# Attention on 32-row float32r slices instead of 128-row bfloat16 pieces, in a transformer block on one core

## The chip, the cores and the metric

The kernel runs on one core of one Trainium2 chip. The metric is the device time in microseconds of one execution; three runs of the kernel before gave 805.25 (median), 802.18 and 806.52.

## What is computed

One block with adaptive layer normalisation, on an input of 2 sequences x 1024 tokens x 128 features, all in float32. Cut to what matters here:

```
h = layernorm(x) * (1 + ca) + sa
q = h @ wq;  lat = h @ w_down;  k = lat @ wk_up;  v = lat @ wv_up      # 16 heads of 8
q, k = rope(q), rope(k)
scores = q . k / sqrt(8)
allowed = page(key) <= page(query)                                     # pages of 32 tokens
attn = softmax(where(allowed, scores, min))
x = x + ga * ((attn @ v) @ wo)
h = layernorm(x) * (1 + cb) + sb
x = x + gb * more_ffn(h)     # 4 rounds of top-2 routing over 4 experts, 128 -> 512 -> 128, gelu
```

The result must be close to float32, so products that the kernel runs at a lower precision are put together from pieces: a number is split into a rounded part and what is left over, and the products of the pieces are added up.

## The kernel before, in words

The kernel has four blocks, one behind the other, with all engines meeting in between: `prep` (line 171), `attention` (421), `project` (753), `ffn` (869). Each engine runs its own written-out order and waits on semaphores.

**prep** goes over four chunks of 512 tokens. TensorE makes q and k (and each with its feature pairs swapped, for the rotation), VectorE rotates them (355 to 362), and ScalarE and GpSimd split each into three bfloat16 pieces: first piece by ScalarE (258), rest by GpSimd (294), second piece by ScalarE (262), third by GpSimd (300). The SP queue stores the three pieces of each side and chunk in DRAM (227), and after the second chunk loads the first two head groups back (`load_group`, 161) in the layout that attention wants, six transfers a group. The block ends when all stores have landed (234).

**attention** works on 8 groups: 2 sequences x 4 groups of 4 heads (`HG`). For each head the 128 rows of the tiles `qs` and `ks` hold six pairs of pieces (`Q_PIECE`, `K_PIECE`; 48 rows), zero rows, 32 rows that mask pages, and 3 rows for the maximum, so one matmul over 128 rows gives masked scores less the row's maximum. Three streams run side by side:

- *Maxima.* For each head, 10 "bins" of up to 512 keys (`BINS`, 61) are filled by TensorE (`fill_bin`, 704: queries on partitions) into one of three banks `mx`, and VectorE reads each with one reduction (588). When a group's 40 bins are read, VectorE merges and splits the maxima in six small steps (602 to 612), TensorE turns them (713), VectorE copies them out (621), and one DMA (498) puts them into the maxima rows of `qs`.
- *Scores and exponentials.* 9 units a group (`UNITS`, 44), each 512 queries wide against one or two key blocks. TensorE makes the scores of each head with keys on partitions (660) into a ring of three banks `st`; ScalarE takes the exponential (562) into `probs`.
- *Values.* TensorE multiplies `probs` with `vs` (681), four heads in four column groups of 32, in float32, in two halves of 256 columns for each unit, into two output banks `ov`; ScalarE copies a finished bank out (568). `vs` has a column of ones, so the sum of the exponentials comes with it.

The order on TensorE is in `body` (724): for each half unit, the scores of two heads of the next unit, a quarter of a part of the bins, the values of half the present unit, the next quarter. The bins run 13 units ahead of the scores (a whole group and `LEAD` = 4), so 57 bins come before the first score. The loop over groups is a hardware loop of two rounds of three groups, with the last two groups written out. SP waits for the first maxima row, issues it, then the feed-forward weights and small tables, then the loads of the third group; later, in each group, a group's loads and a maxima row (500). GpSimd splits the feed-forward weights (539 to 543) and stages `vs`.

Of the kernel before, what the change touches and what calls it, by code (L numbers as in the profile page):

```python
# [32 lines left out]
Q_PIECE = [0, 0, 0, 1, 1, 2]  # L33
K_PIECE = [0, 1, 2, 0, 1, 0]
TERMS = len(Q_PIECE)
ROW_ZERO = TERMS * D
ROW_PAGE = 64
ROW_MAX = P - 3
NPAGE = T // PAGE
MASKED = -3.0e38  # L40
# [4 lines left out]
    [(0, 0, 0, 0, 512)],  # L45
    [(1, 0, 0, 0, 512)],
    [(0, 2, 0, 256, 256), (1, 6, 256, 256, 256)],
    [(0, 1, 0, 128, 384), (0, 3, 384, 384, 128)],
    [(1, 1, 0, 0, 512)],
    [(1, 2, 0, 0, 512)],  # L50
    [(1, 3, 0, 0, 512)],
    [(1, 4, 0, 0, 512)],
    [(1, 5, 0, 128, 384), (1, 7, 384, 384, 128)],
]
NU = len(UNITS)
FIRST_UNIT = [0, 1]
LAST_UNIT = [3, NU - 1]
# [15 lines left out]
GROUP_BINS = [(h, n) for h in range(HG) for n in range(len(BINS))]  # L73
NBINS = len(GROUP_BINS)
NB = NBINS + 1
LEAD = 4
CHAIN = 6
TURN_AFTER = 7
PARTS = [GROUP_BINS[u * NBINS // NU:(u + 1) * NBINS // NU] for u in range(NU)]
BEFORE = [u * NBINS // NU for u in range(NU)]  # L80

# [17 lines left out]
def adaln_block(nc, w, out):  # L99

    with ExitStack() as stack:
# [4 lines left out]
        m.qp = nc.dram_tensor("q_pieces", (3, GROUPS, HG * D, T), BF16).ap()  # L106
        m.kp = nc.dram_tensor("k_pieces", (3, GROUPS, HG * D, T), BF16).ap()
        m.x = m.sb("x_sb", [P, NT, E])
        m.ident = m.sb("ident", [P, P])
        m.identb = m.sb("identb", [P, P], BF16)  # L110
# [19 lines left out]
        with ExitStack() as upto_attention:  # L130
            ma = Mem(nc, upto_attention)
            m.v = ma.sb("v_all", [P, GROUPS, JB, HG * D])
            m.ks = [ma.sb(f"ks{s}", [P, HG, T], BF16) for s in range(SLOTS)]
            m.qs = [ma.sb(f"qs{s}", [P, HG, T], BF16) for s in range(SLOTS)]
# [23 lines left out]
LOADS = [(0, 3), (3, 2), (5, 1)]  # L158


def load_group(sp, m, g, s):

    for first, n in LOADS:
        rows = slice(first * D, (first + n) * D)
        sp.dma_start(m.ks[s][rows, :, :],
                     m.kp[0:n, g].rearrange("c (d h) t -> c d (h t)", d=D)).then_inc(m.qk_in[s], 16)
        one = m.qp[Q_PIECE[first]:Q_PIECE[first] + 1, g].rearrange("c (d h) t -> c d (h t)", d=D)
        sp.dma_start(m.qs[s][rows, :, :], one.broadcast_to([n, D, HG * T])).then_inc(m.qk_in[s], 16)


def prep(nc, m, l):
# [18 lines left out]
    rr = [l.sb(f"rr{s}", [P, CH]) for s in "qk"]  # L190
# [17 lines left out]
    with nc.Block() as block:  # L208

        @block.sync  # L210
        def _(sp):
# [8 lines left out]
            for c in range(NCH):  # L220
# [8 lines left out]
                if c == 1:  # L229
                    sp.wait_ge(pieces_out, 16 * 4)  # L230
                    load_group(sp, m, 0, 0)
                    load_group(sp, m, 1, 1)
# [971 lines left out]
```

## Time and profile before

| | before |
|---|---|
| runs: median (lowest to highest) | 805.25 us (802.18 to 806.52) |
| profiled execution: span from first to last instruction | 804.3 us |
| mean granted TensorE clock | 0.947 |
| TensorE busy | 720.4 us (90%) |
| VectorE busy | 595.7 us (74%) |
| ScalarE busy | 551.1 us (69%) |
| GpSimd busy | 190.9 us (24%) |
| moved by DMA | 20.06 MB |

The profile gives no time of the profiled execution but its span. The stages follow from the first and last instructions of each block: prep to 74 us, attention to 340, projection to some 360, feed-forward to the end. In the rows, PE is TensorE (PEld its weight loads, a line of their own because they overlap the matmuls), DVE VectorE, ACT ScalarE, POOL GpSimd, SPq the DMA-issuing queue of the sync engine. A float32 matmul stands as two records, and matmul ends are modelled, so the starts are what to read.

### The profile page before, as it was taken

How to read it: one execution, taken by the hardware profiler on the slowest of the kernel's cores; microseconds unless marked ns; L12 is line 12 of the kernel's file. 1: busy time of each engine (PE TensorE's matmuls, PEld its weight loads, DVE VectorE, ACT ScalarE, POOL GpSimd, SP SyncE). 2: the span in 40 equal slices, each digit the busy share in tenths (PEclk: the TensorE clock that was granted, in tenths of full speed). 3: DMA queues.
4: the chain of work that ended last, by engine and by line, in shares of the span. 5: the costliest groups of instructions: out<-in, count | busy, mean ns of one | idle time of the engine just before them, and what ended most of it. 6: DMA issues, size and time to landing. Idle time of an engine off the chain costs nothing.

```text
span 804.3 us, 14061 instructions
## 1 busy us (share of the span) xinstructions
PE 720.4 (90%) x4265; PEld 453.4 (56%) x4265; DVE 595.7 (74%) x1148; ACT 551.1 (69%) x958; POOL 190.9 (24%) x152
## 2 busy tenths in 40 slices
PE   4912897999899999977999999999999999999998
PEld 2400132333333333355777777877787777777786
DVE  5752986888688884095687788777887788777876
ACT  2520054766577768825888888888888888888884
POOL 0541033000000000002233333332333333332333
PEclk9965588999999999996999999999999999999999
DMA  9531040110110100000000000000000000000001
GB/s 239 158 119 50 0 131 22 40 38 12 37 30 15 40 4 2 2 1 0 1 2 1 0 1 0 0 0 0 0 0 0 0 0 0 0 0 0 0 0 52
DMA packets 14580, 20.06 MB, mean 25 GB/s; under 512 B 2794, under 2 KB 10474, under 8 KB 13766
## 3 DMA queue, kind: packets, MB, share of 16 engines
q1 hardware_dynamic: 13221, 17.74, 7.4%
q10 hardware_dynamic: 1312, 1.74, 0.8%
q8 instruction: 26, 0.43, 0.2%
q14 instruction: 21, 0.16, 0.1%
HBM read 15.08 MB, written 4.19 MB: 24 GB/s over the span
## 4 chain that ended last, share of the span: by engine, by line
PE 47%; issue 3%; DVE 2%; ACT 1%; POOL 0%; POOLq 0%; DVEq 0%
PE y L951 8%; PE y L953 7%; PE y L952 7%; PE hid L939 7%; PE hid L941 7%; PE hid L940 7%; PE pcw L969 4%; PE plog L959 2%; ACT gel_hi L1011 1%; DVE cw L1086 0%; DVE cw L1084 0%; DVE gel_lo L1042 0%; POOL cur L1135 0%; POOL cur_lo L1123 0%; DVE hdiff L1076 0%
## 5 line engine op out<-in xcount | busy, mean ns | idle before, releaser
L1042 DVE TENSOR_TENSOR gel_lo<-gel,gel_hi 128x512 fp32r<-128x512 f32 x257 | 254.0, 1027 | 12.7 <-ACT gel_hi L1011 6.7
L588 DVE TENSOR_REDUCE mcol<-mx 128x1 f32<-128x512 f32 (+2 forms) x320 | 193.0, 634 | 62.1 <-PE mx L704 59.1
L562 ACT ACTIVATE probs<-st 128x512 f32<-128x512 f32 x288 | 155.7, 596 | 98.8 <-PE st L660 98.3
L1010 ACT ACTIVATE gel<-hid,b_sb 128x512 f32<-128x512 f32 x257 | 178.1, 693 | 38.6 <-PE hid L941 19.5
L1011 ACT ACTIVATE gel_hi<-hid,b_sb 128x512 fp32r<-128x512 f32 x257 | 176.7, 688 | 0.0
L1135 POOL TENSOR_TENSOR cur<-cur,part 128x512 f32<-128x512 f32 x64 | 105.1, 1643 | 279.7 <-DVE part L1093 279.7
L704 PE MATMUL mx<-ks,qs 125*128 125x512 bf16 (+3 forms) x384 | 120.1, 361 | 40.0 <-PEq L208 32.1
L951 PE MATMUL y<-gel_hi,w_hi 128*128 128x512 f32 x256 | 111.9, 437 | 0.0
L1093 DVE SCALAR_TENSOR_TENSOR part<-y,b_sb,cwb 128x512 f32<-128x512 f32 x64 | 48.1, 751 | 77.3 <-PE y L953 77.3
L939 PE MATMUL hid<-cur_hi,w_hi 128*128 128x512 f32 x259 | 103.7, 400 | 0.0
L941 PE MATMUL hid<-cur_hi,w_lo 128*128 128x512 f32 x259 | 103.5, 400 | 0.0
L940 PE MATMUL hid<-cur_lo,w_hi 128*128 128x512 f32 x259 | 103.5, 400 | 0.0
L704 PEld LDWEIGHTS mx<-ks,qs 125*128 125x128 bf16 x384 | 33.1, 99 | 122.6 <-DVE mcol L588 58.6
L952 PE MATMUL y<-gel_hi,w_lo 128*128 128x512 f32 x256 | 101.5, 396 | 0.0
L953 PE MATMUL y<-gel_lo,w_hi 128*128 128x512 f32 x256 | 101.4, 396 | 0.0
L660 PE MATMUL st<-qs,ks 128*128 128x512 bf16 (+3 forms) x384 | 88.4, 331 | 9.0 <-DMA qs<-mrow 5.3
L681 PE MATMUL ov<-probs,vs 128*32 128x256 f32 (+1 forms) x1280 | 93.2, 373 | 0.4 <-ACT probs L562 0.4
L951 PEld LDWEIGHTS y<-gel_hi,w_hi 128*128 128x128 f32 x256 | 48.5, 189 | 19.1 <-DVE gel_lo L1042 11.4
L941 PEld LDWEIGHTS hid<-cur_hi,w_lo 128*128 128x128 f32 x259 | 49.5, 191 | 11.8
L940 PEld LDWEIGHTS hid<-cur_lo,w_hi 128*128 128x128 f32 x259 | 49.5, 191 | 11.7
L939 PEld LDWEIGHTS hid<-cur_hi,w_hi 128*128 128x128 f32 x259 | 49.2, 190 | 11.8
L953 PEld LDWEIGHTS y<-gel_lo,w_hi 128*128 128x128 f32 x256 | 48.2, 188 | 11.9
(144 smaller groups left out, 620.2 us busy)
## 6 DMA issues: line engine op xcount, KB each, us to landing
ks<-in_k_rows SPq DMA_DIRECT2D x3, 640.0 KB
qs<-in_q_rows SPq DMA_DIRECT2D x3, 616.0 KB
q_pieces<-pieces_q SPq DMA_DIRECT2D x4, 384.0 KB, 4.8
k_pieces<-pieces_k SPq DMA_DIRECT2D x4, 384.0 KB, 6.1
ks<-k_pieces SPq DMA_DIRECT2D x8, 192.0 KB
qs<-q_pieces SPq DMA_DIRECT2D x8, 192.0 KB
x_sb<-in_x SPq DMA_DIRECT2D x4, 256.0 KB, 5.0
ks<-k_pieces SPq DMA_DIRECT2D x8, 128.0 KB
```

Source lines behind the costliest of these rows:

```text
L562: nc.scalar.activation(probs[u % SLOTS][:, h, :], st[:, (HG * u + h) % ST_RING, :], ACT.Exp, scale=SCALE).then_inc(exp_done, 1)
L588: nc.vector.tensor_reduce(mcol[a % SLOTS][:, h, slot:slot + step * (len(blocks) - 1) + 1:step], mx[:, at % MX_RING, 0:len(blocks) * keys]. ...
L704: mm = nc.tensor.matmul(mx[:, at % MX_RING, x * keys:(x + 1) * keys], m.qs[s][0:ROW_MAX, h, t * P:(t + 1) * P], m.ks[s][0:ROW_MAX, h, k0:k ...
L939: nc.tensor.matmul(h, m.w1_hi[:, e, f], cur_hi[:, c, :], start=True, stop=False)
L940: nc.tensor.matmul(h, m.w1_hi[:, e, f], cur_lo[:, c, :], start=False, stop=False)
L941: nc.tensor.matmul(h, m.w1_lo[:, e, f], cur_hi[:, c, :], start=False, stop=True).then_inc(hid_ok, 1)
L951: nc.tensor.matmul(o, m.w2_hi[:, x, :], gel_hi[s % RING][:, :], start=first, stop=False)
L952: nc.tensor.matmul(o, m.w2_lo[:, x, :], gel_hi[s % RING][:, :], start=False, stop=False)
L953: nc.tensor.matmul(o, m.w2_hi[:, x, :], gel_lo[s % RING][:, :], start=False, stop=last).then_inc(y_ok, 1)
L1010: nc.scalar.activation(gel[s % RING][:, :], hid[s % RING][:, :], ACT.Gelu_apprx_tanh, bias=bias)
L1011: nc.scalar.activation(gel_hi[s % RING][:, :], hid[s % RING][:, :], ACT.Gelu_apprx_tanh, bias=bias).then_inc(gel_ok, 1)
L1042: nc.vector.tensor_tensor(gel_lo[s % RING][:, :], gel[s % RING][:, :], gel_hi[s % RING][:, :], ALU.subtract).then_inc(lo_ok, 1)
```

## The change

Before, a head takes the whole 128 rows of TensorE. After, a head takes 32 rows, and four heads lie in one tile of 128 rows:

- q and k are split into two float32r pieces instead of three bfloat16 ones, with three products (24 rows) instead of six (48); then 2 rows for the maximum (two pieces) and 4 rows that mask the pages of the diagonal block alone. Whole blocks above the diagonal are never computed, so only the 128 columns of a block's own diagonal need the mask rows; a matmul that has both is split in two (128 columns on 30 rows, the others on 26, or 24 for maxima).
- The pieces go to DRAM in the final row layout: three stores for each side and chunk, and two DMAs that lay down the constant rows there. A group's load is two DMAs of 128 x 1024 float32.
- Maxima: a bin is done for two heads at once, in two row groups into two banks, and VectorE reads both with one reduction: 20 double bins a group, a ring of two double banks. The six small VectorE steps become one merge on VectorE and two steps on GpSimd. Four DMAs instead of one put the maxima rows in place.
- Scores: 10 units a group, each of one half of the sequence; two of them 256 columns wide. The ring stays at three banks.
- Values: one pass over up to 512 columns for each block of a unit, one output bank instead of two.
- Order on TensorE in a step: scores of heads 0 and 1, a double bin, head 2, the values of the step before, a double bin, head 3. Bins run 14 units ahead. All loops are written out. SP issues the weights, the small tables and the third group's loads ahead of the first maxima row.

The diff, cut to its core:

```diff
-Q_PIECE = [0, 0, 0, 1, 1, 2]
-K_PIECE = [0, 1, 2, 0, 1, 0]
+Q_PIECE = [0, 0, 1]
+K_PIECE = [0, 1, 0]
...
+    (0, [(0, 0, 0, 512)]),
+    (0, [(1, 0, 128, 384), (3, 384, 384, 128)]),
+    (0, [(2, 0, 256, 256)]),
+    (1, [(0, 0, 0, 512)]),
+    (1, [(1, 0, 0, 512)]),
+    (1, [(2, 0, 0, 512)]),
+    (1, [(3, 0, 0, 512)]),
+    (1, [(4, 0, 0, 512)]),
+    (1, [(5, 0, 128, 384), (7, 384, 384, 128)]),
+    (1, [(6, 0, 256, 256)]),
...
+PAIRS = HG // 2
+NBINS = len(BINS) * PAIRS
 LEAD = 4
-TURN_AFTER = 7
+TURN_AFTER = 2 * PAIRS
...
-            m.ks = [ma.sb(f"ks{s}", [P, HG, T], BF16) for s in range(SLOTS)]
+            m.ks = [ma.sb(f"ks{s}", [P, T], F32R) for s in range(SLOTS)]
...
+    for dst, src in ((m.ks[s], m.kp), (m.qs[s], m.qp)):
+        sp.dma_start(dst[:, :].bitcast(F32), src[g].rearrange("h r t -> (h r) t")).then_inc(m.qk_in[s], 16)
...
+                    for term, x in enumerate(which):
+                        sp.dma_start(rows[:, D * term:D * (term + 1), at],
+                                     pieces[side][:, c, x, :].bitcast(F32)).then_inc(pieces_out, 16)
...
-    ST_RING, MX_RING = 3, 3
+    ST_RING, PROBS, MX_RING = 3, 3, 2
...
-    ov = l.ps("ov", [P, 2, CH])
-    mx = l.ps("mx", [P, MX_RING, CH])
+    ov = l.ps("ov", [P, CH])
+    mx = l.ps("mx", [P, MX_RING, PAIRS, CH])
...
+                for h in range(HG):
+                    n = 2 * JB
+                    sp.dma_start(m.qs[s][HROWS * h + ROW_MAX:HROWS * h + ROW_MAX + 2, :].bitcast(F32),
+                                 mrow[n * h:n * (h + 1), :]).then_inc(mrow_in[s], 16)
...
+            load_group(sp, m, 2, 2)
+            for g in range(GROUPS):
+                max_rows(g)
+                if g >= 1 and g + 2 < GROUPS:
+                    sp.wait_ge(st_done, HG * NU * g)
+                    load_group(sp, m, g + 2, (g + 2) % SLOTS)
...
+            for k in range(STEPS):
                 for h in range(HG):
+                    exps(k, h)
+                if k >= 1 and (k - 1) % NU in LAST_UNIT:
+                    keep_output(k - 1)
...
+                if n >= ST_RING:
+                    pe.wait_ge(exp_done, n + 1 - ST_RING)
+                for j, off, q0, nq in blocks:
+                    own = P if j // TPC == c else 0
+                    for rows, x, w in ((ROW_END, 0, own), (ROW_PAGE, own, nq - own)):
+                        if w:
+                            mm = nc.tensor.matmul(st[:, n % ST_RING, off + x:off + x + w],
+                                                  m.ks[s][r0:r0 + rows, j * P:(j + 1) * P],
+                                                  m.qs[s][r0:r0 + rows, c * CH + q0 + x:c * CH + q0 + x + w],
+                                                  start=True, stop=True)
...
+                pe.wait_ge(exp_done, HG * (k + 1))
...
+                if u in FIRST_UNIT and 2 * g + c > 0:
+                    pe.wait_ge(ov_read, 2 * g + c)
+                for j, off, q0, nq in blocks:
                     for h in range(HG):
+                        mm = nc.tensor.matmul(ov[32 * h:32 * h + 32, q0:q0 + nq],
+                                              vs[s][:, j, h, :], probs[k % PROBS][:, h, off:off + nq],
...
+                if at >= MX_RING:
+                    pe.wait_ge(bin_read, at + 1 - MX_RING)
                 blocks, keys, _, _ = BINS[b]
                 for x, (t, k0) in enumerate(blocks):
+                    own = P if k0 + keys == (t + 1) * P else 0
+                    for rows, y, w in ((ROW_MAX, 0, keys - own), (ROW_END, keys - own, own)):
+                        for i in range(PAIRS):
+                            r0 = HROWS * (2 * pair + i)
+                            if w:
+                                mm = nc.tensor.matmul(mx[:, at % MX_RING, i, x * keys + y:x * keys + y + w],
+                                                      m.qs[s][r0:r0 + rows, t * P:(t + 1) * P],
+                                                      m.ks[s][r0:r0 + rows, k0 + y:k0 + y + w], start=True, stop=True)
...
+            for unit in range(NU + LEAD):
+                for pair in range(PAIRS):
+                    bins(unit, pair)
+            for k in range(STEPS):
+                scores(k, 0)
+                scores(k, 1)
+                bins(k + NU + LEAD, 0)
+                scores(k, 2)
+                if k >= 1:
+                    weigh(k - 1)
+                bins(k + NU + LEAD, 1)
+                scores(k, 3)
+            weigh(STEPS - 1)
```

## Rows read from the trace of the kernel before

**Rows 1.** The page: span, DMA rate in 40 slices, costly groups (busy us, mean ns).

```profile
span 804.3 us, 14061 instructions
...
GB/s 239 158 119 50 0 131 22 40 38 12 37 30 15 40 4 2 2 1 0 1 2 1 0 1 0 0 0 0 0 0 0 0 0 0 0 0 0 0 0 52
...
L588 DVE TENSOR_REDUCE mcol<-mx 128x1 f32<-128x512 f32 (+2 forms) x320 | 193.0, 634 | 62.1 <-PE mx L704 59.1
...
L704 PEld LDWEIGHTS mx<-ks,qs 125*128 125x128 bf16 x384 | 33.1, 99 | 122.6 <-DVE mcol L588 58.6
...
L951 PEld LDWEIGHTS y<-gel_hi,w_hi 128*128 128x128 f32 x256 | 48.5, 189 | 19.1 <-DVE gel_lo L1042 11.4
```

**Rows 2.** Stretches: length, busy us of each engine, granted clock, DMA share, GB/s.

```profile
85.00:105.00 20.00, 17.89 (x45) 4.19 (x44) 19.90 (x44) 0.00 (x0) 0.00 (x0) 0.50 0.02 5
...
105.90:316.00 210.10, 196.02 (x1743) 73.45 (x1741) 167.35 (x315) 141.41 (x263) 16.89 (x22) 0.98 0.11 34
...
316.00:340.00 24.00, 22.67 (x248) 7.61 (x244) 0.00 (x0) 22.13 (x43) 0.00 (x0) 1.00 0.01 1
```

**Rows 3.** Timeline (start, length): attention's first matmuls and its last.

```profile
74.77 4.70 PE L704 MATMUL mx<-ks,qs 125*128 125x128 bf16 x12 [32.06 <-PEq L208]
...
337.98 1.08 PE L681 MATMUL ov<-probs,vs 128*32 128x256 f32 x24 [0.39 <-ACT probs L562]
```

**Rows 4.** Timeline of steady attention: half a unit, and one exponential behind its scores.

```profile
241.39 0.64 PE L681 MATMUL ov<-probs,vs 128*32 128x256 f32 x8
...
241.96 0.39 PE L704 MATMUL mx<-ks,qs 125*128 125x512 bf16 x1
...
242.19 0.60 PE L660 MATMUL st<-qs,ks 128*128 128x384 bf16 x4
...
242.62 0.38 PE L704 MATMUL mx<-ks,qs 125*128 125x512 bf16 x1
...
242.94 0.64 PE L681 MATMUL ov<-probs,vs 128*32 128x256 f32 x8
...
249.92 0.60 PE L660 MATMUL st<-qs,ks 128*128 128x512 bf16 x2
...
250.34 1.08 ACT L562 ACTIVATE probs<-st 128x512 f32<-128x512 f32 x2 [0.38 <-PE st L660]
```

**Rows 5.** Timeline of the SP queue: maxima rows of two successive groups.

```profile
166.48 0.79 SPq L498 DMA_DIRECT2D qs<-mrow  x1
...
195.77 0.80 SPq L498 DMA_DIRECT2D qs<-mrow  x1
```

**Rows 6.** Timeline of the tail, without maxima work: scores of two half units.

```profile
329.61 0.61 PE L660 MATMUL st<-qs,ks 128*128 128x512 bf16 x2
...
330.72 0.60 PE L660 MATMUL st<-qs,ks 128*128 128x512 bf16 x2
```

**Rows 7.** End of prep: a stretch, and the SP queue's last issue.

```profile
50.00:60.00 10.00, 0.00 (x0) 0.00 (x0) 2.14 (x11) 0.00 (x0) 0.00 (x0) 0.50 0.48 159
...
55.07 11.86 SPq L227 DMA_DIRECT2D k_pieces<-pieces_k  x1
```

**Rows 8.** Groups by shape from 75 to 102 us: reductions of 512 and 384 columns.

```profile
L588 DVE TENSOR_REDUCE mcol<-mx 128x1 f32<-128x512 f32 x28 | 17.2, 678 | 0.0
...
L588 DVE TENSOR_REDUCE mcol<-mx 128x1 f32<-128x384 f32 x10 | 5.1, 546 | 0.0
```

**Rows 9.** Timeline of the first scores and exponentials.

```profile
105.94 0.88 PE L660 MATMUL st<-qs,ks 128*128 128x512 bf16 x3
...
106.42 1.57 ACT L562 ACTIVATE probs<-st 128x512 f32<-128x512 f32 x3 [30.49 <-PE st L660]
...
107.07 0.88 PE L660 MATMUL st<-qs,ks 128*128 128x512 bf16 x2 [0.26 <-ACT probs L562]
```

**Rows 10.** Waits from 105 to 316 us: total us, times, longest.

```profile
PE st L660 <- DMA qs<-mrow: 5.3, 6, 1.1
PE mx L704 <- DMA qs<-q_pieces: 4.0, 1, 4.0
```

More of the change, by code:

```diff
@@ L578, in _, with exps @@
-            exps(0, 0, 0)
-            all_groups(act, body)
+            def exps(k, h):
+                u = k % NU
+                n = sum(b[3] for b in UNITS[u][1])
+                act.wait_ge(st_done, HG * k + h + 1)
+                if h == 0 and k >= PROBS:
+                    act.wait_ge(pv_done, k + 1 - PROBS)
+                nc.scalar.activation(probs[k % PROBS][:, h, 0:n], st[:, (HG * k + h) % ST_RING, 0:n], ACT.Exp,
+                                     scale=SCALE).then_inc(exp_done, 1)
@@ L651, in _, with scores @@
+            for g in range(GROUPS):
+                for n in range(NBINS):
+                    if n == 1 and g >= 1:
+                        merge(g - 1)
+                    if n == TURN_AFTER and g >= 1:
+                        keep_rows(g - 1)
+                    read_bin(g, n)
+            merge(GROUPS - 1)
+            keep_rows(GROUPS - 1)
         @block.tensor
         def _(pe):
-            def scores(i, a, u, h):
-                s, n = a % SLOTS, HG * (NU * gnum(i, a) + u) + h
+            def scores(k, h):
+                g, u = divmod(k, NU)
+                s, n, r0 = g % SLOTS, HG * k + h, HROWS * h
+                c, blocks = UNITS[u]
@@ L663, in scores @@
[L663 to L679 removed]
+                    pe.wait_ge(m.qk_in[s], 32 * uses(g))
@@ L724, in body @@
-            def body(i, a):
-                for u in range(NU):
-                    nxt, side = following(i, a, u), part_at(i, a, u)
-                    for half in range(2):
-                        if exists(*nxt[:2]):
-                            scores(*nxt, 2 * half)
-                            scores(*nxt, 2 * half + 1)
-                        if exists(*side[:2]):
-                            part(*side, 2 * half)
-                        weigh(i, a, u, half)
-                        if exists(*side[:2]):
-                            part(*side, 2 * half + 1)
-                    if side[2] == 0 and exists(i, a + 1) and not exists(*side[:2]):
-                        turn_maxima(i, a + 1)
@@ L740, in _ @@
-            nc.tensor.sem_inc(st_done, ST_CREDIT)
-            nc.tensor.sem_inc(exp_done, EXP_CREDIT)
-            nc.tensor.sem_inc(pv_done, PV_CREDIT)
-            nc.tensor.sem_inc(ov_read, OV_CREDIT)
-            for a, parts in ((0, NU), (1, LEAD)):
-                for p in range(parts):
-                    for quarter in range(4):
-                        part(0, a, p, quarter)
-            for h in range(HG):
-                scores(0, 0, 0, h)
-            all_groups(pe, body)
+                    own = P if k0 + keys == (t + 1) * P else 0
```

397 lines of the change are left out of this document (130 added, 267 removed).

## The prediction, made before the changed kernel ran

> **What bounds the kernel now.** I start from the page: the span, and the costliest groups [rows 1]. Shares over the span can't say what a change to one stage is worth, so the stretches come next [rows 2]. The edits lie in two stages: the preparation, up to 74.8 us, and attention, up to 339.1 us (the last value pass starts at 337.98 and takes 1.08) [rows 3]. The 465 us behind that are projection and feed-forward, which no edit touches; I take them over unchanged.
>
> Within attention TensorE has hardly any free time: from 105.9 to 316 us it is busy for 196.0 of 210.1, VectorE for 167.4, ScalarE for 141.4 [rows 2]. Busy isn't streaming, so I read the order of starts. Half a unit takes 1.55 us (241.39 to 242.94): the values for 0.57, a maxima matmul for 0.23, two score matmuls for 0.43, a maxima matmul for 0.32 [rows 4]. A 512-column matmul streams in about 0.22, so 0.1 of the last term is the gap ahead of the value matmuls, and I put the same 0.1 behind them. The bound is this one row of work on one engine. A head group takes 29.3 us (166.48 to 195.77) [rows 5]. Without maxima work the half costs 1.11 (329.61 to 330.72) [rows 6].
>
> Ahead of it lie two other bounds. From 50 to 60 us no compute engine does more than 2 us of work, while the store queue moves 159 GB/s; the last key pieces are issued at 55.07 and hold it for 11.86 us [rows 7], behind twelve loads of eight to 24 rows each, and the block ends when they land. From 74.8 to 105.9 VectorE reads maxima without a pause (19.90 of 20 us), at a granted TensorE clock of 0.50, the 1.2 GHz level [rows 2].
>
> **The change part by part.** *Preparation.* The third piece goes, with one ScalarE and one GpSimd operation for each side and chunk; the first stores can go a little earlier, which I count at nothing, since the last ones decide. The stores grow from 384 KB to three of 256 KB for each side and chunk; each load shrinks from six partly filled ones to two of 128 partitions x 4 KB (512 KB). After the second chunk, at about 43 us, 2.1 MB of loads and 3.1 MB of stores remain. Bounds: 5.2 MB at 239 GB/s, the best slice [rows 1], is 22 us; at 159, where this queue ran last [rows 7], 33 us. With 2 us to land the block ends at 67 or 78. I take 69, nearer the first, since what drags the queue in the end is small loads on few rows, and those go: **-6 us** (ends -8 and +3). The issues (twelve stores and four loads, 0.8 us each by the nearest row [rows 5]) fit under the transfers.
>
> *Maxima ahead of the first scores.* A double bin has 921 columns on average. A column costs 1.03 ns (678 against 546 ns for 128 fewer), and an instruction 0.09 us more than its columns (17.2/28 - 0.53) [rows 8]: 1.04 us. 28 of them are 29 us, against 31.2 now (74.77 [rows 3] to 105.94 [rows 9]): **-2**. On the SP queue the weights and small loads go ahead of the first maxima row, and are through long before it. On GpSimd the weight splitting, nearly all of its 16.9 us [rows 2], stands between the first and second splitting of maxima; that leaves it some 5 us to spare (splitting from 21 to 38 us after the start, second merge at 42).
>
> *Steady attention, VectorE.* 20 x 1.04 + 0.4 for merge and row copy = 21.2 us a group, against 24.1 (193.0/8 [rows 1]). The five small steps that go to GpSimd or vanish lie beside TensorE's work now: nothing.
>
> *Steady attention, TensorE.* The value matmuls keep their columns (4608 a group); half as many calls save gaps: 0.57 twice now, 0.88 + 0.1 once then, where 0.88 is two passes of 512 columns, each twice the (0.57 - 0.1)/2 of a 256-column pass less a fixed 0.03. Scores and maxima run on 32 rows. If two row groups stream at once, a step would need some 2.2 us of TensorE. But the order written out makes a longer chain. Let head 3 of step k-1 start at 0. Its exponential starts 0.42 later (249.92 to 250.34 [rows 4]), and TensorE goes on 0.65 after that start (106.42 to 107.07 [rows 9]). Head 2 of step k waits for just that: the score ring stays three deep, and heads 0 and 1 and the first double bin are long through. Then, each on the same in-order engine: head 2, 0.22; gap, 0.1; values, 0.88; gap, 0.1; second double bin, 0.23; head 3 starts. Sum 2.60. Matmuls split in 128 + 384 columns and the two-block units add about 0.1: 2.7. The two units of 256 columns save 0.8 each: 8 x 2.7 + 2 x 1.9 = 25.4 us a group, above VectorE's 21.2, so VectorE waits.
>
> 66 steps have maxima work: 168 us. 14 have none: 2.4 each, less three narrow units: 31; a step of the tail gets longer (2.4 against twice 1.11), since an exponential's wait stands where score matmuls stood. The early load of the third group takes away the one wait for it, 4.0 us [rows 10]; that lies in the 233.1 below. Added waits: there is one output bank instead of two. The copy stands behind head 3's exponential: 0.42 + 0.49 (one exponential's pitch, 1.57 - 1.08 [rows 4, 9]) + 0.65 = 1.56 after head 3, where the values want the bank at 1.39: 0.17 x 16 = 3. A maxima row needs four issues in place of one; with 0.80 for one [rows 5] the last goes up to 2.4 later; it is due two steps, 5.4 us, after the turn; waiting now costs 5.3 in six cases [rows 10]. I take 5, ends 0 and 15. Getting the clock up: 3. In all 168 + 31 + 11 = 210, against 233.1 now (105.94 to 339.1): **-23 us**.
>
> *Row tiles.* No row shows 32-row matmuls. What rows show is columns: eight passes of 256 columns for four heads in 0.57 [rows 4], so four at a time. The Trainium skill's page "TensorEngine Tiling (Array Packing)", under "Key Properties", says that tiles load and multiply in parallel and that a change of tiling mode drains the engine. By it the sum stands; without overlap it is the first rival. *Weight loads.* A bf16 load takes 99 ns, a 4-byte one 189 [rows 1]; there are 144 a group in place of 96. The Trainium skill's "TensorE: Matmul & The Clock Gate", "Weight-path perf modes", says that the fast load is for types other than fp32, and that speaks against this change. If each of the 1152 loads laid its added 90 ns bare, that were 104 us and the time 877. In my chain most lie in the 1.07 us of waiting.
>
> Sum: 804.3 - 6 - 2 - 23 = **773 us**. For the profiled execution I have its span of 804.3 alone, 0.1% under the median of the runs, 805.25, so I correct nothing.
>
> **Rivals.** (1) *The row groups don't overlap, or the loads hold up short matmuls.* Heads 0, 1 and the first bin (0.9) still fit in the 1.07 of waiting, but the second bin takes 0.43 and more where it is split: 2.9 a step, 0.2 x 80 more: 790. For it: nothing here shows row tiles. Against: the column tiles. (2) *The new waits eat it*: stores at 159 GB/s (+9), maxima rows late (+10), dearer gaps: 797 to 805. For it: rows are waited for now, 0.9 us a time. Against: their lead grows. (3) *Slower: the clock.* At 1.2 GHz what streams doubles: 0.64 + 0.65 + 0.43 + 0.1 + 1.8 + 0.1 + 0.43 = 4.1 against 2.6. The gain of 31 is spent after 21 such steps; half the stage low gives 830, all of it 885. For it: from 85 to 105 us the clock stays at 0.50 with TensorE busy for most of the time, since it waits between bins; my step streams 1.8 of 2.7 us. Against: the tail waits too (0.9 of 1.11 streams) and stands at 1.00 [rows 2].
>
> **How the numbers follow.** Forecast 0.58 (752 to 786), rival 1 0.17, rival 2 0.12, the clock 0.13. The forecast's low end: stores at their best (-2), no late rows (-5), no clock ramp (-3), no split extras (-8), no bank waits (-3). The range reaches over rival 1 and most of 2: 752 to 803; it leaves out the clock and a rest. What runs of this kernel can tell from no change is 0.5%, 4 us: faster is the forecast, rival 1 and a quarter of 2, 0.78; same 0.08; slower 0.14.
>
> **What would show it.** Right: head 2's score matmuls released by ScalarE once a step; steps of 2.6 to 2.8 us; VectorE busy under 85% in attention, waiting for TensorE; maxima matmuls of two heads starting within 0.1 us of each other; attention starting at 66 to 72 us; the clock at 1.00 from the fifth step on. Wrong: VectorE without idle time (the chain is shorter than I count), score matmuls waiting for the row transfer in every group, clock rows below 0.9, or stores that end after 78 us. A stage behind attention that isn't 465 us long would say that something outside this sum moved.

## Result and profile after

The changed kernel takes 921.85 us (median of 4 runs, 921.05 to 923.56) against 805.0 before: ratio 1.146, 95% interval 1.143 to 1.148. The change makes it slower by 117 us; the forecast was 773. Lines of the page, with the granted clock in 40 slices:

```profile
span 920.0 us, 12557 instructions
...
PEclk9955555555555555555859999899998999999999
...
L546 DVE TENSOR_REDUCE mcol<-mx 128x2 f32<-128x1024 f32 (+3 forms) x160 | 172.1, 1115 | 156.9 <-PE mx L628 156.7
```

The stretches that answer to [rows 2, 7] (length, busy us of each engine, granted clock, DMA share, GB/s):

```profile
50.00:60.00 10.00, 0.18 (x4) 0.21 (x8) 0.79 (x4) 0.23 (x1) 0.22 (x1) 0.50 0.90 347
60.00:90.60 30.60, 20.45 (x115) 12.84 (x115) 28.30 (x30) 1.06 (x1) 11.51 (x20) 0.50 0.35 105
90.60:400.00 309.40, 274.86 (x1655) 129.36 (x1655) 146.10 (x146) 144.56 (x296) 12.48 (x28) 0.50 0.05 19
400.00:438.20 38.20, 31.99 (x166) 12.08 (x162) 0.00 (x0) 18.91 (x39) 0.00 (x0) 0.50 0.00 1
```

The granted clock is 0.50, the 1.2 GHz level, from the first maxima matmul to the last value pass; before it was 0.98 to 1.00 behind 105.9 [rows 2]. VectorE works 146 of 309 us there and waits for TensorE. The timeline shows a step of 4.49 us (240.01 to 244.50; start, length), which answers to [rows 4]:

```profile
240.01 1.93 PE L608 MATMUL ov<-probs,vs 128*32 128x512 f32 x8
241.88 0.79 PE L628 MATMUL mx<-ks,qs 24*128 24x512 f32 x2
241.89 1.21 PE L589 MATMUL st<-qs,ks 26*128 26x512 f32 x3
242.48 0.63 PE L628 MATMUL mx<-ks,qs 24*128 24x384 f32 x4
243.78 0.79 PE L589 MATMUL st<-qs,ks 26*128 26x512 f32 x1 [0.67 <-ACT probs L521]
244.50 1.08 PE L608 MATMUL ov<-probs,vs 128*32 128x512 f32 x4
...
243.13 2.07 ACT L521 ACTIVATE probs<-st 128x512 f32<-128x512 f32 x4 [1.93 <-PE st L589]
```

The SP queue issues the maxima rows 44.4 us apart, a head group's time, against 29.3 [rows 5]:

```profile
169.39 2.56 SPq L447 DMA_DIRECT2D qs<-mrow  x4
213.78 2.97 SPq L447 DMA_DIRECT2D qs<-mrow  x4
```

Where the 116 us between the two spans lie:

| part | before | after | difference |
|---|---|---|---|
| up to the first maxima matmul | 74.8 | 59.8 | -15.0 |
| maxima ahead of the first scores | 31.2 | 30.8 | -0.4 |
| attention behind the first scores (to 339.1 and 438.2) | 233.1 | 347.6 | +114.5 |
| projection, feed-forward, end | 465.2 | 481.8 | +16.6 |

The last row is a surprise: no edit touches that code. In the records the feed-forward's TensorE work lasts 433.2 us before (367.6 to 800.8) and 447.6 after (468.8 to 916.5).

### The profile page after: what moved, and what is told of

It reads as the page before. It is cut to its first block and busy times, and to the rows that moved or that the text cites. A ratio compares the mean times of both kernels' runs of the same rounds, so it can differ in the third digit from the quotient of the medians.

```text
span 920.0 us, 12557 instructions
## 1 busy us (share of the span) xinstructions
PE 811.8 (88%) x4137; PEld 528.3 (57%) x4137; DVE 564.9 (61%) x947; ACT 546.2 (59%) x982; POOL 181.6 (20%) x160
## 5 line engine op out<-in xcount | busy, mean ns | idle before, releaser
L521 ACT ACTIVATE probs<-st 128x512 f32<-128x512 f32 (+1 forms) x320 | 157.8, 557 | 212.5 <-PE st L589 212.2
L546 DVE TENSOR_REDUCE mcol<-mx 128x2 f32<-128x1024 f32 (+3 forms) x160 | 172.1, 1115 | 156.9 <-PE mx L628 156.7
L952 DVE TENSOR_TENSOR gel_lo<-gel,gel_hi 128x512 fp32r<-128x512 f32 x257 | 249.4, 1009 | 19.6 <-issue 6.8
L589 PE MATMUL st<-qs,ks 30*128 30x128 f32 (+4 forms) x576 | 154.9, 527 | 40.5 <-ACT probs L521 39.4
L589 PEld LDWEIGHTS st<-qs,ks 30*128 30x128 f32 (+1 forms) x576 | 94.3, 308 | 83.6 <-ACT probs L521 68.8
L608 PE MATMUL ov<-probs,vs 128*32 128x512 f32 (+3 forms) x768 | 141.1, 848 | 0.5 <-ACT probs L521 0.5
L628 PEld LDWEIGHTS mx<-ks,qs 24*128 24x128 f32 (+1 forms) x576 | 72.5, 312 | 115.4 <-issue 85.4
L628 PE MATMUL mx<-ks,qs 30*128 30x128 f32 (+4 forms) x576 | 110.0, 499 | 25.7 <-PEq L198 16.4
```

The costliest lines, as they stand in the source:

```text
L521: nc.scalar.activation(probs[k % PROBS][:, h, 0:n], st[:, (HG * k + h) % ST_RING, 0:n], ACT.Exp, scale=SCALE).then_inc(exp_done, 1)
L546: nc.vector.tensor_reduce(mcol[g % 2][:, pair * 2:pair * 2 + 2, slot:slot + step * (len(blocks) - 1) + 1:step], mx[:, at % MX_RING, :, 0:l ...
L589: mm = nc.tensor.matmul(st[:, n % ST_RING, off + x:off + x + w], m.ks[s][r0:r0 + rows, j * P:(j + 1) * P], m.qs[s][r0:r0 + rows, c * CH + ...
L628: mm = nc.tensor.matmul(mx[:, at % MX_RING, i, x * keys + y:x * keys + y + w], m.qs[s][r0:r0 + rows, t * P:(t + 1) * P], m.ks[s][r0:r0 + r ...
L952: nc.vector.tensor_tensor(gel_lo[s % RING][:, :], gel[s % RING][:, :], gel_hi[s % RING][:, :], ALU.subtract).then_inc(lo_ok, 1)
```

## Experiments: the clock

Each run of this section is one execution, beside runs of the kernel before on the same chip (medians 805.8 to 806.4, single ones 805.5 to 807.4); differences of 2 or 3 us say nothing. The theory: matmuls on 24 to 30 of 128 rows leave so much of the array unused that the clock stays down. The rivals: the waits on exponentials keep it down, or only the cold start does.

**e1_warm** starts the stage warm.

```
+            pe.wait_ge(m.qk_in[0], 32)
+            pe.wait_ge(mrow_in[0], 16 * HG)
+            for i in range(60):
+                nc.tensor.matmul(st[:, i % ST_RING, :], m.ks[0][:, 0:P], m.qs[0][:, 0:CH], start=True, stop=True)
             for k in range(STEPS):
```

> The kernel after, with 60 matmuls of 512 columns on all 128 rows (their results are overwritten) ahead of the first score matmuls; nothing else differs. At the granted clock of 0.50 they take 60 x 0.43 = 26 us, less if the clock rises on the way. Theory A (matmuls on 24 to 30 of the 128 rows don't hold the clock up, however many there are): the clock rises to 1.00 during the 60 and falls back to 0.50 within the first steps; a step stays at 4.5 us, time about 922 + 15 to 26 = 937 to 948. Theory B (it is TensorE's waiting for the exponentials, once a step, that keeps the clock down): it falls back as well, same time. Theory C (the stage merely starts cold, and 4.5 us steps keep it cold): the clock stays at 1.00, steps of 2.6 to 2.8 us, main stage 80 x 2.7 = 216 instead of 348, time about 922 - 132 + 15 = 805.

935.84 us. The stretches:

```profile
100.00:105.00 5.00, 5.00 (x24) 4.13 (x22) 0.00 (x0) 0.00 (x0) 0.00 (x0) 1.00 0.00 0
105.00:110.00 5.00, 4.58 (x37) 3.35 (x39) 2.94 (x3) 3.19 (x7) 0.00 (x0) 0.91 0.00 0
110.00:115.00 5.00, 4.31 (x29) 2.03 (x25) 2.96 (x3) 1.88 (x5) 0.00 (x0) 0.50 0.01 3
```

The 60 full matmuls (89.73 to 106.2) bring 1.00; the clock falls at 109.1, 3 us into the steps behind them, and stays down to the end of attention. The cold start falls as a cause.

**e2_rows128** changes the rows and leaves order and waits. Its scores add up four heads, so its output is not the block's; only its times are of use here.

```
-    m.ks[s][r0:r0 + rows, j * P:(j + 1) * P], m.qs[s][r0:r0 + rows, ...]
+    m.ks[s][:, j * P:(j + 1) * P], m.qs[s][:, ...]
(the same in fill_bin)
-MASKED = -3.0e38
+MASKED = -3.0e37
```

> The kernel after, with score and maxima matmuls on all 128 rows of the tiles in place of one head's 32 (each then sums over four heads; the mask constant is ten times smaller so that the sum stays finite). The same columns, the same order of work, the same waits; only that no two of them overlap any more. Theory A (rows in use decide): the clock goes to 1.00; a step has 4 x 0.22 of scores, 4 x 0.2 of maxima and 0.9 of values, and its chain is 0.42 + 0.65 + 0.22 + 0.1 + 0.88 + 0.1 + 0.43 = 2.8 us; main stage 225, time 922 - 348 + 225 = 800. Theory B (the waiting decides) and theory C (the cold start decides): it stays at 0.50; a step then streams 5.2 us and its chain is 0.64 + 0.65 + 0.43 + 0.3 + 1.8 + 0.3 + 0.86 = 5.0, main stage 400 to 420, time 975 to 995.

833.93 us: the clock comes back, and most of the loss goes. The page's clock line:

```profile
PEclk9955599999999999995999998999999999899999
```

The maxima rows on its SP queue, 32.7 us a group:

```profile
158.44 2.56 SPq L447 DMA_DIRECT2D qs<-mrow  x4
...
191.14 2.98 SPq L447 DMA_DIRECT2D qs<-mrow  x4
```

No two of its score or maxima matmuls overlap, and still it is 88 us faster than the change. But at 1.00 a group takes 32.7 us, not the 28 of the expectation and more than the 29.3 of before. Most steps take 3.0 to 3.3 us, those with columns split in 128 + 384 or more up to 4.4.

Full rows alone don't lift the clock, though. Ahead of its first scores e2 runs maxima on all 128 rows with waits for VectorE between them, and stays at 0.50 for 30 us, as the kernel before does from 85 to 105 us [rows 2]:

```profile
60.00:90.00 30.00, 28.72 (x93) 21.61 (x93) 24.62 (x24) 0.75 (x1) 6.47 (x15) 0.50 0.33 106
```

**e3_order** moves the values ahead of the wait instead (the output copy moves with them).

```
                 bins(k + NU + LEAD, 0)
+                if k >= 2:
+                    weigh(k - 2)
                 scores(k, 2)
-                if k >= 1:
-                    weigh(k - 1)
```

> The kernel after with the order of a step changed: scores of heads 0 and 1, first maxima, values of step k-2 in place of k-1, scores of head 2, second maxima, scores of head 3; the output copy moves one step later with it. TensorE then no longer waits behind a fresh exponential ahead of head 2 with the values queued behind it. Theory A (rows decide): the clock stays at 0.50; what a step streams at that clock is 1.8 of values, and 0.43 for each of three or four groups of overlapping matmuls, with gaps 3.6 to 4.0 us instead of 4.5; main stage 290 to 320, time 865 to 895. Theory B (the waiting decides): the waits go, the clock rises to 1.00, a step is bound by VectorE at 2.12 us, main stage 175 to 190, time 750 to 765.

919.72 us: neither. The granted clock stays at 0.50 and the step at 4.4 us, though TensorE's records now cover 96.5 of 100 us. Its timeline shows what the edit left: a head's scores still wait for an exponential once a step, since the ring stays three deep.

```profile
200.00:300.00 100.00, 96.46 (x543) 49.09 (x539) 49.08 (x49) 46.57 (x93) 2.18 (x8) 0.50 0.07 23
...
241.72 0.79 PE L589 MATMUL st<-qs,ks 26*128 26x512 f32 x1 [0.25 <-ACT probs L521]
...
246.21 0.28 PEld L589 LDWEIGHTS st<-qs,ks 26*128 26x128 f32 x1 [0.55 <-ACT probs L521]
```

The record of such a matmul lasts 0.79 us, while on one row group a new one starts every 0.43 at this clock (34.49 / 80 in m1 below), so busy isn't streaming here. The next run has a step in the change's own order, all of 512-column matmuls and without waits: 3.03 us at 0.50 (128.87 to 131.90). So e3 is not a run without waits, and its 4.4 us are not all work.

**m1_clock** leaves the kernel's work out and runs matmuls alone, nine stretches of the kinds below.

```
+    r0 = 32 * (i % 4)
+    nc.tensor.matmul(b[i % 4][:, :], fr[r0:r0 + 26, 0:P], fr[r0:r0 + 26, CH:2 * CH], start=True, stop=True)
```

> The kernel's work is left out: x is copied to the output, and TensorE runs nine stretches of matmuls without any wait inside, some 8 us of pause between them. 1: 80 matmuls of 512 columns, float32r, 128 rows. 2: 240 on four row groups of 26 rows in turn. 3: 80 on one row group. 4: 60 value matmuls, float32, four column groups. 5: eight times a step of the kernel after, without its waits. 6: the same with all 128 rows in scores and maxima. 7: 60 full ones, then 320 on four row groups. 8: 60 full ones, then 14 steps. 9: 60 full ones, then 100 on one row group. Theory A (rows in use decide): 1.00 is reached in 1 and 6; 2 and 3 stay at 0.50 though TensorE never waits; 7 and 9 rise in their full part and fall back behind it; 5 and 8 end at 0.50. Theory B (waiting decides): every stretch reaches 1.00, since none waits. Theory C (a cold start decides): 2, 3 and 5 stay at 0.50, but 7, 8 and 9 keep 1.00 to their ends. Four row groups should stream at once, one 512-column matmul starting every 0.43 / 4 = 0.11 us at 0.50, or every 0.055 at 1.00.

Timeline: stretch 2 (four row groups), 3 (one), the values of two steps in a row of stretch 5, then the last part of 7 (four row groups, behind 60 full matmuls), one step of 8, and the last part of 9 (one row group, behind 60 full ones):

```profile
41.46 15.89 PE L146 MATMUL bank<-fr 26*128 26x512 f32 x240 [6.72 <-DVE slow L132]
64.10 34.49 PE L151 MATMUL bank<-fr 26*128 26x512 f32 x80 [6.75 <-DVE slow L132]
...
128.87 1.94 PE L165 MATMUL bank<-wide,x_sb 128*32 128x512 f32 x8
...
131.90 1.94 PE L165 MATMUL bank<-wide,x_sb 128*32 128x512 f32 x8
...
200.38 18.45 PE L185 MATMUL bank<-fr 26*128 26x512 f32 x320
...
242.09 1.07 PE L195 MATMUL bank<-wide,x_sb 128*32 128x512 f32 x8
243.09 0.50 PE L197 MATMUL bank<-fr 26*128 26x512 f32 x2
...
243.43 0.39 PE L197 MATMUL bank<-fr 26*128 26x512 f32 x1
...
243.76 1.07 PE L195 MATMUL bank<-wide,x_sb 128*32 128x512 f32 x8
...
288.65 40.70 PE L204 MATMUL bank<-fr 26*128 26x512 f32 x100
```

And its stretches: one row group; the step without waits at its start and later; the step without waits behind a warm start; one row group behind a warm start:

```profile
64.10:98.60 34.50, 34.49 (x80) 25.77 (x80) 0.00 (x0) 0.00 (x0) 0.50 0.00 1
...
131.00:134.00 3.00, 3.00 (x20) 0.69 (x24) 0.00 (x0) 0.00 (x0) 0.50 0.00 0
134.00:144.80 10.80, 10.79 (x99) 3.04 (x99) 0.00 (x0) 0.00 (x0) 0.98 0.01 2
...
242.00:265.00 23.00, 23.00 (x220) 6.39 (x219) 0.00 (x0) 0.00 (x0) 1.00 0.01 1
...
300.00:329.00 29.00, 29.00 (x69) 22.09 (x68) 0.00 (x0) 0.00 (x0) 0.50 0.00 0
```

Four row groups overlap fully: one matmul every 0.058 us (18.45 / 320) at 1.00. One row group, busy for 34.5 us without a gap, never rises, and brings a warm clock down. But four at once rise and hold, and so do steps in the order of the changed kernel (all of 512 columns) once nothing waits in them, at 1.67 us a step (242.09 to 243.76). So the theory in its first form falls for stretches 2, 5, 7 and 8, and "waiting alone" falls for 3 and 9. The step's four cases side by side:

| | with the kernel's waits | without waits |
|---|---|---|
| 24 to 30 rows | 0.50 (the change, e1, e3) | 1.00 (m1, stretches 5, 8) |
| 128 rows | 1.00 (e2) | 1.00 (m1, stretch 6) |

For the step it takes both, few rows and pauses. Either can do alone elsewhere: one row group stays low without a pause (stretch 3), and full-row maxima with pauses stay low as well (e2 from 60 to 90 us). What fits these cases is the share of the array that works over time; this is argued from them, and no run measures it. e2 has rows in use, and because its matmuls don't overlap also less time free; it doesn't separate those two.

**e4_fill** and **e5_waitfill** keep the row groups and add full-array matmuls; both also start warm as e1 does. **e7_maxrows** has maxima matmuls alone on full rows (e2's edit of fill_bin).

```
e4 (in scores, behind the wait; order of e3)
+                if h == 2:
+                    for i in range(2):
+                        nc.tensor.matmul(st[:, n % ST_RING, :], m.ks[s][:, 0:P], m.ks[s][:, 0:CH], start=True, stop=True)
e5 (ahead of scores(k, 2), behind a wait for the bank pair)
+                for i in range(3):
+                    nc.tensor.matmul(mx[:, at % MX_RING, i % 2, :], m.ks[g % SLOTS][:, 0:P], m.ks[g % SLOTS][:, 0:CH], start=True, stop=True)
```

> The kernel after with values of step k-2 as in e3, the 60 full matmuls ahead of the first scores as in e1, and in each step two more matmuls of 512 columns on all 128 rows (keys by keys, overwritten by the scores of head 2 that follow them into the same bank). Useful work is as in e3. Theory A (what counts is how much of the array works over time, rows in use times streaming; m1's stretches on four row groups and its steps without waits rose to 1.00, one row group alone never did): the fillers hold 1.00; a step is bound by VectorE's 2.12 us and TensorE's 1.67 + 0.44 + 0.1, so 2.2 to 2.3 us, main stage about 180, time 922 - 348 + 180 + 15 = 770 (760 to 785). Theory B (any wait on another engine within a step brings it down, whatever the array does): it falls back to 0.50 as in e1, a step is e3's 4.45 and 0.9 of fillers, time 960 to 1005.

> The kernel after, its own order of a step, with the 60 full matmuls first and three matmuls of 512 columns on 128 rows between the first maxima and the scores of head 2, where TensorE waits for the exponential; they go to the bank pair that the second maxima overwrite. Every wait of the kernel after stays. Theory A (share of the array at work over time): the clock stays at 1.00, 3 x 0.22 fit in the wait of 0.65, a step is the chain of the prediction with a little more, 2.7 to 2.9 us, main stage 215 to 232, time 922 - 348 + 222 + 15 = 811 (800 to 825). Theory B (waits): 0.50, steps of 4.5 to 5, time 935 to 980.

> The kernel after with the maxima matmuls alone on all 128 rows (they sum over four heads, the mask constant is ten times smaller), scores on 32 rows as before, the order and the waits unchanged. Theory A (share of the array at work over time): at 0.50 a step now holds 1.8 of values and four maxima matmuls of 0.43 on full rows, so the clock rises within the first steps; at 1.00 the chain is 0.42 + 0.65 + 0.22 + 0.1 + 0.88 + 0.1 + 0.43 = 2.8 us; main stage 225 to 245, time 800 to 820. Theory B (waits): it stays at 0.50, a step is 4.5 + 0.43 and more, time 955 to 990.

956.69, 1027.41 and 868.45 us. e4's page shows a clock that goes up and down:

```profile
PEclk9955865856665958695587999989999999989999
```

e7's is up for most of the stage, with one fall at 266 us, and falls again in its tail:

```profile
PEclk9955589999996899558699999999989999999999
```

The direction of the theory holds (more of the array at work, more time at 1.00: e1 none, e4 part, e7 most, e2 all behind its first steps), the sizes don't. In e4 most full steps that ran at 1.00 still took 3.3 to 3.7 us where I put 2.2 to 2.3. Its timeline, here of two steps near the end without maxima work, shows two things that I had left out: the fillers take 0.67, not 0.44 (and the values ahead of them 1.0 for 0.88 of streaming), and the scores wait for an exponential again:

```profile
411.76 1.07 PE L611 MATMUL ov<-probs,vs 128*32 128x512 f32 x8
412.75 0.73 PE L587 MATMUL st<-ks 128*128 128x512 f32 x2
413.42 0.56 PE L592 MATMUL st<-qs,ks 26*128 26x512 f32 x4
414.59 0.55 PE L592 MATMUL st<-qs,ks 30*128 30x128 f32 x2 [0.62 <-ACT probs L521]
```

e5's 1027.41 lies outside both of its theories. Three fillers at 0.50 are 1.3 us, more than the wait of 0.65 that should hide them, and they bring a wait of their own: they need the bank pair that VectorE has yet to read, which the timeline shows as 0.89 us of idle time ahead of them:

```profile
250.74 1.65 PE L640 MATMUL mx<-ks 128*128 128x512 f32 x3 [0.89 <-DVE mcol L546]
```

So e5 changed the waits too, and says little of the clock. Fillers in these two places cost more than they gave.

**e8_full2, e9_scorerows2, e10_maxrows2** are e2, scores alone on full rows, and e7, each in the order of e3 and with the idle instructions of the next section. As in e2, the output of e8 and e9 is not the block's.

> e2 (scores and maxima on all 128 rows, sums over four heads, smaller mask constant) with the order of e3 (values of step k-2) and 202 idle instructions on VectorE behind its last maxima work, where it waits for nothing else. In e2 a head group took 32.7 us at a granted clock of 1.00 with TensorE busy 49.5 of 50 us. If that busy time is work (128-column pieces start 0.11 us apart there, twice their columns), the order gives little: 31 to 32.7 us a group, attention 250 us behind the first scores. If it still holds one wait of 0.5 us a step, 28 to 29 us a group and 225 us. For the theory of the granted clock (it follows how much of the array works over time) both should stay at 1.00. The feed-forward stage: 433 us if VectorE's code position alone matters, 447.6 if ScalarE's does. Total 785 (the wait goes) to 820 (it doesn't), 14 more if the stage behind stays long.

> e8 with the maxima matmuls back on 32-row groups: scores alone on 128 rows (sums over four heads). TensorE's work in a step at 1.00: 0.88 of scores, 0.88 of values, 0.44 of maxima, changes of tiling 0.3: 2.5 us, so 25 us a group if the clock holds, attention 205 us behind the first scores, total 770. What works of the array is 0.88 + 0.88 + a quarter of 0.88 in 2.5 us; e4 had about as much of 2.2 and went up and down between the two levels, so the clock is the open point: at 0.50 a step is about 4.6, and a mean of 0.75 gives 3.3 us a step and 830.

> e7 (maxima matmuls alone on 128 rows) with the order of e3 and VectorE's idle instructions as in e8. e7's granted clock was 1.00 through most of the stage and a group took 33.7 us; its tail, without maxima work, was at 0.55. With the values of step k-2 the wait on the exponential should go: 27 to 30 us a group at 1.00, total 785 to 810; if the 33.7 us were work of TensorE and not a wait, no change, 850 (868 less 14 of the stage behind, if that goes).

819.64, 842.03 and 862.47 us. The new order is worth nothing in e8 (33.2 us a group against 32.7 in e2) and nothing in e10 (34.5 against e7's 33.7, where both stand at 1.00). In e9 the clock came up only at 164.6 us; from there a group takes 32.9 us at 1.00, as its stretch shows:

```profile
180.00:220.00 40.00, 38.97 (x299) 22.10 (x303) 26.87 (x29) 25.32 (x52) 0.87 (x3) 1.00 0.09 31
```

So in all three a step at 2.4 GHz takes 3.3 to 3.5 us on average, whichever part uses full rows. Where overlap should save, time goes at each change of tiling. In e9's records of one step the maxima matmuls (start 231.03) are followed by scores 0.43 later, scores by maxima 0.32 later (232.04 to 232.36), and maxima by values 0.43 later (232.36 to 232.79), each around a 512-column matmul that streams in 0.22: 0.1 to 0.2 us for a change. A weight load laid bare at the change would look the same; no run tells the two apart. How the change's own step would run at 1.00 no run shows, since nothing held the clock there.

## Experiments: the stages around attention

**e6_pad and a1_place** move code and do nothing else; **b2_shift** does the same to the kernel before.

```
a1 (VectorE, attention; e6 has 437 like waits on ScalarE as well)
             keep_rows(GROUPS - 1)
+            for i in range(403):
+                v.wait_ge(bin_read, turn_at(GROUPS - 1) + 1)
b2 (VectorE, attention, behind all groups)
+            for p in range(107):
+                v.wait_ge(mchain, 1)
```

The expectations count instructions where the code has waits: 403 waits are 202 instructions, 437 are 219, and 107 are 54.

> The kernel after with idle instructions alone: 202 more on VectorE behind its last maxima work (waits that are long fulfilled) and 219 more on ScalarE ahead of its first exponential, each in time in which that engine has nothing to do. They put the code of the feed-forward loop where it stands in the kernel before (VectorE: the same place; ScalarE: the same place but for 256 instructions). The feed-forward stage took 447.6 us after and 433.2 before with the same code, and the instruction queue fetched code in each of its passes after, not before. Theory P (the place of the loop in the code decides whether it is fetched again in each pass): 433 us for the stage, time 907 to 908. Theory Q (the stage is longer because of the clock, or of what the stage before leaves): no change, 921 to 923.

> The kernel after with nothing but 202 idle instructions on VectorE behind its last maxima work, which put the feed-forward loop at the same place of VectorE's code as in the kernel before; 202 x 0.077 us = 16 us of a 50 us stretch in which VectorE has nothing to do. Theory P (VectorE's place alone): feed-forward stage 433 in place of 447.6, 921.9 - 14.5 = 907.4 (906 to 909). Theory Q (ScalarE's place counts too): 912 to 922.

> The kernel before with 54 idle instructions on VectorE behind its last maxima work (4 us, while it has nothing to do), so that the feed-forward loop begins at instruction 721, the same place within 256 instructions as in the kernel after (465). Theory P: the loop's code is fetched again in every pass, the feed-forward stage goes from 433 to 447 us, time 819 to 820. Theory Q: nothing changes, 804 to 807.

e6: 925.34 us (4 runs), but its feed-forward stage took 433.2; the ScalarE instructions waited for the first scores and put off the first exponential from 91.5 to 110.8, an error of mine that hid the gain. a1: 907.49 us (4 runs), ratio to before 1.126 (1.124 to 1.128), 14.4 less than the change as it stands. b2: 820.25 us. The timeline of VectorE at the start of a pass of the feed-forward loop, in the kernel after:

```profile
585.92 0.75 DVE L1003 SCALAR_TENSOR_TENSOR part<-y,b_sb,cwb 128x512 f32<-128x512 f32 x1 [1.80 <-PE y L863]
589.02 3.47 DVE L952 TENSOR_TENSOR gel_lo<-gel,gel_hi 128x512 fp32r<-128x512 f32 x4 [2.35 <-issue]
```

The same place in a1:

```profile
586.02 0.75 DVE L1005 SCALAR_TENSOR_TENSOR part<-y,b_sb,cwb 128x512 f32<-128x512 f32 x1 [1.80 <-PE y L865]
586.69 5.09 DVE L954 TENSOR_TENSOR gel_lo<-gel,gel_hi 128x512 fp32r<-128x512 f32 x4
```

In the kernel after VectorE waits 2.35 us for nothing that a semaphore shows. The DMA view of its 575 to 600 us has the reason (packets, MB, share of 16 engines); in a1 that stretch has no packet at all:

```profile
q14 instruction: 3, 0.02, 0.4%
```

And b2, the kernel before with its code moved, at 470 to 500 us (VectorE waits 2.39 us there):

```profile
q14 instruction: 4, 0.03, 0.4%
```

Code is fetched again as each further pass of the loop begins. That it was VectorE's place in the code is shown in both directions: 54 idle instructions cost the kernel before 14 us (one execution), 202 give them back to the change. The waits themselves are 6.8 of the 14.5 us (2.35, 2.28 and 2.21 at 589.0, 699.1 and 809.1). Behind two of them the granted clock falls too, to a mean of 0.91 from 588.8 to 628.8 us and from 668.8 to 708.8, where the kernel before and a1 hold 1.00; that can be most of the rest. The other 2 us of the last row of the table are the projection, 27.8 us for 25.7: its first 6 us run at the low clock, and in e2 and e3, where the clock is up as it begins, it takes 25.8.

**b1_rows** does the preparation's idea on the kernel before: full rows in DRAM, one load for a side.

```
-        sp.dma_start(m.ks[s][rows, :, :], m.kp[0:n, g]...)      (three of each, for LOADS)
+    for dst, src in ((m.ks[s], m.kp), (m.qs[s], m.qp)):
+        sp.dma_start(dst[0:TERMS * D, :, :], src[:, g].rearrange("c (d h) t -> c d (h t)", d=D))
-                    sp.dma_start(dst..., pieces[side][:, c, :, :])
+                    for first, k in LOADS:      (terms first to first + k, q's by broadcast)
+                        sp.dma_start(dst[first:first + k]..., src)
```

> The kernel before with one idea of the change's preparation alone: the DRAM copy of the pieces holds all six terms of a side (three stores for each side and chunk in place of one, twice the bytes), so that a group's side comes in one load of 48 rows x 8 KB in place of three. Attention and all behind it are those of before. Theory R (it was the loads on few rows that held the preparation back; the change's own ended at 59.8 us in place of 74.8 with the same bytes stored): the first maxima matmul goes up to 60 to 63 us, attention keeps 233 us and its clock of 1.00, time 805 - 13 = 792 (790 to 795). Theory S (what ended earlier in the kernel after was due to the third piece that it no longer makes): no gain or a loss, 803 to 812.

797.46 us (5 runs, 796.3 to 798.11), ratio to before 0.989 (0.987 to 0.990): 8.7 us less than before, clear of the noise if under 2%, and less than the 13 expected. The timeline:

```profile
69.87 5.30 PE L706 MATMUL mx<-ks,qs 125*128 125x128 bf16 x14 [25.79 <-PEq L204]
```

Attention starts 4.9 us earlier (74.77 [rows 3]), a third of the 15; the wait for the third group's rows, 4.0 us [rows 10], is gone too, as it should by one load in place of three: its attention takes 228.7 us behind the first scores (101.5 to 330.1) against 233.1. The other 10 us of the change's preparation belong to its larger packets, its missing third piece or both; these weren't taken apart.

## Why the prediction was wrong

*The step that failed* is the granted clock. The sum took all of attention at 1.00, with "Getting the clock up: 3" as the only price, and the range left the clock out; it stood at 0.50 from the first maxima matmul to the last value pass, and attention behind the first scores took 347.6 us for my 210. With the clock back in e2 88 of the 117 us are back. The ground for leaving it out was "Against: the tail waits too (0.9 of 1.11 streams) and stands at 1.00". I weighed streaming time and didn't count rows. That tail streams on all 128 rows [rows 6]; a score or maxima matmul of the change uses 24 to 30. m1 puts it plainly: 34.5 us of streaming without a pause on one row group leave the clock at 0.50. The other row was nearer and I discounted it: from 85 to 105 us full-row matmuls with waits stay at 0.50 [rows 2]. The rival itself named what came: "all of it 885"; with the stages behind left out the run gives 921.85 - 16.6 = 905. That this is so near is in part luck: attention took 26 us more than the rival's 210 + 80 x 1.4 = 322, and the preparation 9 less than the sum had. That few rows together with the waits keep the clock down is shown for this step by e1, e2 and m1; what exactly the clock goes by stays open.

*The chain* was right as a chain. TensorE goes on 0.65 behind the exponential's start in the trace of after (243.13 to 243.78), and head 2 waits for it, as said. At 1.2 GHz the rival put 0.64 + 0.65 + 0.43 + 0.1 + 1.8 + 0.1 + 0.43 = 4.1. Measured: from the start of the second maxima to head 3's exponential 1.25 (241.88 to 243.13) for my 0.43 + 0.64 = 1.07, then 0.65, head 2 and the gap 0.72 for 0.53, values and the gap 1.87 for 1.9. The sum is 4.49. In the records head 3 starts beside the second maxima, but one of those two matmuls is on head 3's own row group, and on one row group matmuls follow each other (0.43 apart in m1's stretch 3); so I read the two terms together. What came on top is some 0.2 us in each of two places.

*At 2.4 GHz* no run shows the change's step, so whether 2.6 to 2.7 us would have held stays open. The 3.3 us of e2, e8 and e9 are steps with more full-row work and can't decide it. An estimate from parts that ran at 1.00: values 1.00 and second maxima 0.33 (m1, 242.09 to 243.09 to 243.43), 0.42 to the exponential and 0.65 (my rows), head 2 to the values 0.42 (411.34 to 411.76 in e4's records) make 2.8 us, 0.2 above the chain. What I undersized at either clock are the changes of tiling, 0.1 to 0.2 each where I had two gaps of 0.1 (e9), and the split columns: 128-column pieces start 0.11 us apart in e2's records, twice their streaming time, and in the kernel after one step in each group takes 5.67 us instead of 4.49 (209.3 to 215.0), where I had "about 0.1" for all of it. What the Trainium skill's "TensorEngine Tiling (Array Packing)", "Key Properties", says of tiles that work in parallel holds here (0.058 us for each of four in turn), and the 0.1 to 0.2 us fit its drain at a change of mode, which I priced too low.

*Weight loads*: the mean of a load is 308 and 314 ns in attention (189 was the 4-byte row [rows 1]), but the loads of a set of row groups start 3 to 7 ns after one another in the records, so they don't add up. The chain leaves no room for the 104 us of bare loads; a part of its 0.2 us extras can be loads.

*Preparation* was better than either end: 59.8 where I had 67 to 78. I took 239 GB/s, "the best slice" [rows 1], for the queue's best; a slice of 20 us averages over idle time, and the queue ran at 347 from 50 to 60 us. Of the 15 us that it gained, the small loads are a third by b1.

*Maxima ahead*: 30.8 us for my 29. A double-bank reduction takes 1.115 us on average, not 1.04. *Late maxima rows*, 5 in the sum: the one wait for them that the profile shows is 1.1 us, ahead of the first scores; at the slower pace this says nothing of 2.4 GHz.

*VectorE* with idle time, head 2 released by ScalarE and a start of two heads' maxima within 0.1 us (241.877 and 241.881) came as listed; none of them told of the clock. The line that did was my own last test, "clock rows below 0.9".

*The 465 us taken over unchanged* weren't: 14.5 of the 16.6 came with code fetched again, through VectorE's code in attention having shrunk by 202 instructions.

## What to carry to other kernels

Before giving TensorE smaller or fewer-row matmuls, ask what the granted clock will do: relief of the busiest engine can halve its speed, and the loss is then far above what the packing saves (here a group took 44.4 us instead of 29.3). Look at the rows in use and at the time spent streaming, not at busy time: the runs here fit that, though none proves it. When a stage that nobody touched moves, look at the instruction queue before looking for contention; and take a queue's best rate from a stretch in which it is full, not from a page slice.

## What was not expected of the hardware

- TensorE streaming without a gap on 26 rows for 34.5 us stays at the 1.2 GHz level, and 60 full matmuls ahead don't help: 100 such matmuls took 40.7 us, 0.41 each. Four row groups in turn run at 2.4 GHz.
- A loop's place in VectorE's code decides whether the code is fetched in each pass: 2.2 to 2.4 us without a releaser at the pass's start, three times, and 13 to 14.5 us over the stage, in two kernels. Shifting it by 54 or 202 instructions turns it on and off. Why those places and not others stays open.
- Between matmuls on row groups, on the full array and on column groups 0.1 to 0.2 us pass beyond the streaming each time at 1.00 (e9); whether that is the change itself or a weight load stays open.
